# Four graph layers on one core: the products of the negated edge mask, one head at a time instead of two

## The reference

```
h = max(layernorm(x), 0);  x = x + attention(h, adj)        # 4 heads of 32, edges where adj > 0.5
h = max(layernorm(x), 0);  x = x + relations(h, adj)        # max over 7 relations
h = max(layernorm(x), 0);  x = x + convolution(h, adj)
h = max(layernorm(x), 0);  x = x + laplace(h, adj)          # softplus at the end
```

```
e    = leaky_relu(d[i] + s[j], 0.2), and -1e9 where adj[i, j] <= 0.5
out  = softmax(e, over j) @ (h @ W[head]) + bias
```

## Time and profile before

| | |
|---|---|
| time, median of three runs | 764.88 us (763.68 to 766.92) |
| the profiled execution | 766.7 us, span 764.9 us |
[...]
| busy: PE, PEld | 695.8 us (91%), 569.7 us (74%) |
| busy: DVE, ACT, POOL | 581.3 us (76%), 458.3 us (60%), 301.1 us (39%) |
| matmuls at L1235 | 1536, busy 54.7 us |
| matmuls at L1249 | 3072, busy 101.4 us |

### The profile page before, as it was taken

How to read it: one execution, slowest core, us unless ns; L and a number is a source line. 1 busy time by engine, 2 the same in 40 slices (tenths; PEclk the granted TensorE clock), 3 DMA queues, 4 the chain that set the end, 5 groups by cost and what they waited for, 6 DMA issues and landing times. The chain is left out here.

```text
span 764.9 us, 20772 instructions
## 1 busy us (share of the span) xinstructions
PE 695.8 (91%) x7890; PEld 569.7 (74%) x7890; DVE 581.3 (76%) x1730; ACT 458.3 (60%) x1137; POOL 301.1 (39%) x359
## 2 busy tenths in 40 slices
PE   0357999999999999999999999999999999999844
PEld 0256777969697887969697978879696979787543
DVE  1658588888888888888888888887888888786330
ACT  0174566666757676666667576766667576754332
POOL 0215163543624453545435344525445253343310
PEclk9988999999999999999999999999999999999977
DMA  7000202020200202020201002020202010000000
GB/s 207 14 2 2 70 3 70 2 83 3 79 7 9 76 2 84 2 84 2 83 3 61 24 3 84 1 85 2 84 3 83 3 53 19 15 3 15 0 15 14
DMA packets 28796, 27.84 MB, mean 36 GB/s; under 512 B 1493, under 2 KB 20506, under 8 KB 28698
## 3 DMA queue, kind: packets, MB, share of 16 engines
q1 hardware_dynamic: 25344, 25.17, 10.6%
q10 hardware_dynamic: 3354, 1.35, 0.9%
HBM read 22.31 MB, written 4.19 MB: 35 GB/s over the span
## 5 line engine op out<-in xcount | busy, mean ns | idle before, releaser
L363 POOL TENSOR_TENSOR rstd<-ve,half_neg 128x4 f32<-128x4 f32 x48 | 52.4, 1091 | 257.0 <-DVE ve L1030 161.9
L1249 PEld LDWEIGHTS ps<-part,pos 128*128 128x128 bf16 x3072 | 99.6, 98 | 3.2 <-DVE pos L942 0.7
L1249 PE MATMUL ps<-part,pos 128*128 128x66 bf16 x3072 | 101.4, 193 | 0.5 <-DVE pos L942 0.5
L947 DVE SCALAR_TENSOR_TENSOR pos<-ps,neg_s,none 128x512 bf16<-128x512 f32 x128 | 87.2, 745 | 12.5 <-issue 12.5
L1011 DVE TENSOR_REDUCE best<-ps 128x128 f32<-128x896 f32 x64 | 68.5, 1085 | 22.1 <-PE ps L1317 20.2
L608 ACT ACTIVATE side<-ps,sd 128x512 bf16<-128x512 f32 x128 | 76.8, 680 | 3.0 <-DVE pos L942 3.0
L1355 PE MATMUL ps<-y,adj_tr 128*128 128x128 f32 x512 | 70.6, 283 | 2.5 <-ACT y L512 2.5
L1355 PEld LDWEIGHTS ps<-y,adj_tr 128*128 128x128 f32 x512 | 65.0, 199 | 2.8 <-ACT y L512 2.8
L1235 PEld LDWEIGHTS ps<-part,nmask 128*128 128x128 bf16 x1536 | 53.5, 99 | 14.8 <-issue 10.5
L1393 PE MATMUL ps<-u,adj_tr 128*128 128x128 f32 x512 | 61.1, 278 | 2.5 <-ACT u L702 2.5
L1235 PE MATMUL ps<-part,nmask 128*128 128x66 bf16 x1536 | 54.7, 197 | 6.9 <-DVE part L930 6.9
(11 more groups left out here) (168 smaller groups left out, 1619.7 us busy)
## 6 DMA issues: line engine op xcount, KB each, us to landing
adj_in<-in_adj SPq DMA_DIRECT2D x16, 1024.0 KB, 6.0
x_in<-in_x SPq DMA_DIRECT2D x16, 256.0 KB, 6.4
out_y<-y_out SPq DMA_DIRECT2D x16, 256.0 KB, 6.7
w_sb<-in_L_gnn_W ACTq DMA_DIRECT2D x7, 64.0 KB, 5.1
b_sb<-in_L_gnn_b ACTq DMA_DIRECT2D x1, 256.0 KB, 8.9
c_rows<-c_parts ACTq DMA_DIRECT2D x6, 1.5 KB
w0c<-in_L_gnn_W ACTq DMA_DIRECT2D x1, 64.0 KB, 2.9
a_bc<-in_L_gnn_a_src ACTq DMA_DIRECT2D x1, 64.0 KB, 5.7
```

Source lines behind the costliest of these rows:

```text
L363: G.tensor_tensor(rstd[:], ve[:], half_neg[:, 0:T], ALU.pow).then_inc(power, 1)
L947: last = V.scalar_tensor_tensor(pos[0][:, t, :], bank(B_SPREAD[h]), neg_s[:, t, h:h + 1], none[:, t, :], ALU.is_gt, ALU.is_gt)
L1249: last = mm(ps[:, B_HEADS[q] + i // 2, o:o + VAL], pos[h % 2][:, t, i * P:(i + 1) * P], parts[n][:, t, h, :], start=False, stop=(i % 2 == ...
```

## The change

In `no_edges(q)` one matmul over two heads (two runs of 33 columns) becomes two matmuls of one head each (one run of 33 columns), with the same stationary operand. A piece has 96 matmuls in place of 48, a graph 192 in place of 96. Only the first of a bank has the start flag. Waits, order of pieces and results are the same.

```diff
                     for i in range(T):
-                        o = (i % 2) * 2 * VAL
                         for t in range(T):
                             for n in range(PARTS):
-                                mm(ps[:, B_HEADS[q] + i // 2, o:o + 2 * VAL].rearrange("p (h v) -> p h v", h=2)[:, :, GRP:VAL],
-                                   nmask[:, t, i * P:(i + 1) * P], parts[n][:, t, 2 * q:2 * q + 2, GRP:VAL],
-                                   start=(i % 2 == 0 and t == 0 and n == 0), stop=False, skip_group_check=True)
+                                for hh in range(2):
+                                    o = ((i % 2) * 2 + hh) * VAL + GRP
+                                    mm(ps[:, B_HEADS[q] + i // 2, o:o + GRP], nmask[:, t, i * P:(i + 1) * P],
+                                       parts[n][:, t, 2 * q + hh, GRP:VAL],
+                                       start=(i % 2 == 0 and t == 0 and n == 0 and hh == 0), stop=False, skip_group_check=True)
```

## The result

The changed kernel takes 794.21 us (median of 4 runs, 792.49 to 795.59) where the kernel before took 765.69 us beside it: a ratio of 1.0374, 95% interval 1.0341 to 1.0407. The medians differ by 28.5 us. The forecast was 795 us, 3.9% slower.

What follows compares the result with a forecast made beforehand. PE was taken as the only bound from graph 2 on, so added PE time counts one to one. 30 blocks at 0.99 us gave +29.7 us on 764.88: 795 us, 3.9% slower, range 784 to 810 us.

Steps and rivals of the forecast that it cites:

- The price of a pair: In the L1235 blocks, a load and matmul of 33 columns taken as 26 ns, 0.99 us more a block.
- The lower end: At L1235, only columns count: a pair takes 16.7 ns, 0.10 us more a block, +3 us in all.
- the upper end: At L1235, a 33-column pair costs as much as one of 66: 30.0 ns, 1.375 us more a block, +41 us.
- The blocks that don't pay: Two of 32 L1235 blocks cost nothing more: the first at lower clock, and one hidden in graph 1's PE waits.
- The sum: The other 30 blocks at L1235 pay 0.99 us each: +29.7 us on the median of 764.88.
- Rival 1: At L1235, a pair has a floor near 30 ns: +41 to +44 us, 806 to 809 us; chance 0.21.
- rivals 2 and 3: Pair 16.7 ns, only columns count, 768 us, chance 0.05; cheaper floor 17 to 22 ns, 769 to 783 us, chance 0.06.
- Rival 4: Thin blocks lower the granted clock, +22 us on top, about 817 us, or instruction fetch falls behind; chance 0.03.

Runs made afterwards that it cites:

- the half change: Changed kernel with only no_edges(0) split and no_edges(1) as before, one of the two blocks of each graph: 779.8 us, ratio 1.0191.
- DVE's second comparison: Kernel before, with DVE's 128x2048 mask comparison done twice, the first time into a spare tile: 767.7 us, ratio 1.0031.
- the runs of 17 and 48 columns: Kernel before, with one more matmul of 17 or 48 columns, which nobody reads, after each matmul at L1235: 802.4 and 803.5 us.
- blocks twice as long: Changed kernel with an added matmul of 17 columns, which nobody reads, after each of its 3072 matmuls of 33: 869.4 us, ratio 1.1359.

## Why the prediction was right

**The bound.** PE alone sets the turns: in five turns it is busy throughout, from 102 to 690 us it waits for no one, and a turn is 42.23 us throughout. The runs show it by the turn that grew by just its two blocks (1.88 and 1.87 us), by the half change (43.15 us) and by DVE's second comparison, which left the turn at 42.23.

**The price of a pair.** Taken as 26 ns, between ends of 16.7 and 30.0; it measured 25.4 (2.42 and 2.46 us a block). The number was close, but the reason given was a choice by nearness: no row told 26 from 22 or 29, so that it came within 0.6 ns is in good part luck. The cause is a floor of 25.4 ns, flat over the 17, 33 and 48 columns measured, that the trace of before couldn't show, since its shortest dense matmuls have 66 columns. The lower end, which carried the slope on below 66 columns, was wrong by 9 ns, and the upper end by 5. The 0.40 ns a column of the lower end is the rise from 66 to 128 columns, (55 - 30.0) / 62 ns by the earlier trace rows; no run shows it below 66, where 17, 33 and 48 columns all took 25.4 ns. One reading on the way there doesn't hold, though the sum doesn't use it: 128 columns of a load aren't shown to be worth 11 ns, since the row of 87 ns is an f32 load, and f32 loads of 128 columns last 140 ns and more on average in the same trace (140 at L1209, 145 at L1149).

**The blocks that don't pay.** Graph 0's first block at the lower clock (0.50 in both) goes from 2.69 to 2.72 us (52.30 to 55.02), so it costs nothing, as worked out from 28 ns of stream. In graph 1's turn the wait of 0.48 us for DVE is gone, but that for ACT shrank only from 1.43 to 1.23, where I had let the waits take a whole block of 0.99; they gave 0.68. From the first block to graph 2's it was 79.21 us, 1.79 more; the steps had 3 x 0.99 - 0.99 = 1.98.

**The sum.** 30 x 0.99 = 29.7 was forecast. With the measured block it is 30 x 0.935 = 28.1, and the medians differ by 28.5. The time came out nearer (795 to 794.2) than the difference, because the sum was added to 764.88 and the kernel before took 765.69 beside the change: two small errors that cancel.

**The rivals.** Rival 1 (a floor near 30 ns) falls with the runs of 17 and 48 columns; rivals 2 and 3 (16.7, or 17 to 22 ns) fall with the same. The further nanosecond that rival 1 has for operands off an even boundary was my estimate, and no run shows it: the matmuls of the changed kernel read and write from an odd column, the added ones of 17 and 48 from an even one, and both took 25.4 ns. Rival 4's clock did not come in this change: it stayed at 1.00 in all full turns. With blocks twice as long it fell once from 120 to 780 us, and with two loads a matmul again and again (mean over the run 0.90). Its other half, instructions that arrive too late, showed in one turn of the changed kernel at most (484.29 to 528.54, 44.25 us in place of 44.10, with a gap of 0.2 us marked as issue). The two runs of 33 columns that I charged with 1.4 ns a pair cost 0.4 at most, which changed nothing in the sum.

## What to carry to other kernels

On an engine that is busy without a gap, price a changed matmul by the distance between starts, not by its duration or its columns: at L1250 a record lasts 194 ns, and the next starts 30.0 ns on; halving the columns of a 66-column bf16 matmul saved 4.6 of 30 ns, so two halves took 50.8 ns where one whole took 31.4. Before narrow matmuls are multiplied or fused, find the floor of a load-and-matmul pair with a few added ones that nobody reads. And look at the timeline when matmuls with stationary operands of two widths come in turn: here an added one of 17 columns with 32 of 128 stationary columns cost 284 ns (1201.5 - 765.9 us over 1536), with all 128 it cost 24 (802.4 - 765.3 us over 1536); a part of that came with the lower clock (0.71 in the block, 0.50 behind it).

## What the runs showed of the hardware that was not expected

- A stand-alone load of weights ahead of a matmul's own load makes the group 57.4 ns long, whether the matmul has 66 or 33 columns and the load 128 or 32: 26 to 32 ns more than with the matmul's own load alone.
- Matmuls of 128 and 32 (or 64) stationary columns in turn start 110 to 140 ns apart at a granted clock of 1.00, against 25 to 31 ns for one width, though added loads of 32 columns cost no more than those of 128 (803.1 and 803.4 us); 1536 added matmuls made the kernel 57% and 63% slower.
- The granted clock fell to 0.50 with PE busy by the profile all the time, behind 5.5 us of matmuls of 33 columns at 57.5 ns; behind blocks of 4.8 us of 33 and 17 columns at 25.2 ns it stayed at 1.00 from 120 to 780 us but for one, which had a gap of 0.34 us in it.
